# Two attention streams, one core: where VectorE prepares the latents, turns the side bank, and where the feed-forward modulation stands

## The reference, cut to what matters

```
hidden = (tanh(g / 2) + 1) * g * u          (twice silu(g) * u)
y     += w_down.T hidden
modh   = 0.1 * tanh(woa.T o) * (wa2.T x)     (once per item)
```

## Time and profile before

| | |
|---|---|
| three timed runs | 3610.35, 3618.64, 3619.7 us (median 3618.64) |
| profiled execution, its own time | 3609.97 us |
| its span, first to last instruction | 3608.2 us |
| mean granted TensorE clock | 0.957 of full speed |
| busy share of the span | PE 92%, PEld 75%, DVE 67%, ACT 54%, POOL 23% |

### The profile page before, as it was taken

One profiled execution on the slowest core, in us unless ns is written; L12 is line 12 of the kernel. 1 busy time (PEld: TensorE's weight loads), 2 busy tenths in 40 slices (PEclk: granted clock), 3 DMA queues, 4 the chain that ended last, 5 costly groups with the idle time before them and its releaser, 6 DMA issues. The chain is left out here.

```text
span 3608.2 us, 89141 instructions
## 1 busy us (share of the span) xinstructions
PE 3313.0 (92%) x34218; PEld 2701.3 (75%) x34218; DVE 2425.1 (67%) x7923; ACT 1959.2 (54%) x4767; POOL 817.1 (23%) x827
## 2 busy tenths in 40 slices
PE   6888896999999999999999868888979999999999
PEld 5676774888888888888888756766757777777787
DVE  4665654778777777777777535565656767777764
ACT  2444453666666666666666524454545555555553
POOL 2322221222222222222222222222210111111100
PEclk8998997999999999999999978898989999999999
DMA  5000000000000000000000040000000000000000
GB/s 223 1 1 1 1 1 18 14 20 20 20 20 20 20 20 20 20 20 20 20 20 20 8 151 1 1 1 1 1 1 1 1 1 1 1 1 7 4 7 10
DMA packets 51336, 66.83 MB, mean 19 GB/s; under 512 B 4962, under 2 KB 40290, under 8 KB 49378
## 3 DMA queue, kind: packets, MB, share of 16 engines
q1 hardware_dynamic: 50914, 61.13, 5.3%
HBM read 58.56 MB, written 2.56 MB: 17 GB/s over the span
## 5 line engine op out<-in xcount | busy, mean ns | idle before, releaser
L1286 DVE SCALAR_TENSOR_TENSOR d_acc<-d_raw,d_taps,d_acc 128x255 f32<-128x255 f32 (+2 forms) x1152 | 642.9, 599 | 146.2 <-ACT d_raw L1276 132.6
L2355 ACT ACTIVATE s_probs<-s_probs,s_nmax 128x128 f32<-128x128 f32 (+1 forms) x768 | 280.7, 443 | 187.9 <-DVE s_nmax L186 187.3
L1511 ACT COPY d_power<-bank 128x768 f32<-128x768 f32 x320 | 259.0, 809 | 218.7 <-PE bank L1504 218.7
L702 POOL TENSOR_TENSOR a_q<-a_rope 64x512 f32<-64x512 f32 x128 | 164.0, 1281 | 738.7 <-DVE a_rope L692 384.7
L186 DVE CUSTOM_DVE_ANT_0 a_area<-bank,mask 128x128 f32<-128x128 f32 (+1 forms) x512 | 160.3, 355 | 241.8 <-PE bank L720 239.4
L739 ACT ACTIVATE a_area<-a_area,a_nmax 128x128 f32<-128x128 f32 (+1 forms) x512 | 226.6, 444 | 165.2 <-DVE a_nmax L186 164.1
L1274 ACT ACTIVATE d_acc<-bank,d_tap_bias,d_taps 128x256 f32<-128x256 f32 x384 | 196.0, 561 | 166.5 <-PE bank L1255 158.7
L186 DVE CUSTOM_DVE_ANT_0 s_probs<-bank,mask 128x128 f32<-128x128 f32 (+1 forms) x768 | 220.9, 353 | 61.7 <-PE bank L2336 60.6
L765 ACT COPY a_area<-bank 128x512 f32<-128x512 f32 (+1 forms) x260 | 140.1, 578 | 138.7 <-PE bank L756 138.1
L2377 DVE COPY s_probsT<-bank 128x384 f32<-128x384 f32 x192 | 106.0, 555 | 119.9 <-PE bank L2363 117.7
L692 DVE TENSOR_TENSOR a_rope<-bank,a_sinT 32x512 f32<-32x512 f32 x256 | 177.4, 693 | 5.6
(11 more groups left out here) (267 smaller groups left out, 8783.3 us busy)
## 6 DMA issues: line engine op xcount, KB each, us to landing
d_alpha<-d_alpha_rows SPq DMA_DIRECT2D x64, 256.0 KB, 3.5
d_g_decay<-d_running_rows SPq DMA_DIRECT2D x32, 258.0 KB, 3.4
a_w_o<-in_a_w_o SPq DMA_DIRECT2D x2, 2048.0 KB, 16.5
a_area<-in_a_q_nope SPq DMA_DIRECT2D x2, 1536.0 KB, 8.2
x<-in_x SPq DMA_DIRECT2D x8, 256.0 KB, 16.3
d_wk<-in_d_wk SPq DMA_DIRECT2D x1, 2048.0 KB
d_wq<-in_d_wq SPq DMA_DIRECT2D x1, 2048.0 KB
d_wv<-in_d_wv SPq DMA_DIRECT2D x1, 2048.0 KB
```

Source lines behind the costliest of these rows:

```text
L702: nc.gpsimd.tensor_tensor(q[CL:P, n % 2], rope1[CL:P], rope2[CL:P], ALU.add)\
L1286: last = nc.vector.scalar_tensor_tensor(out=acc[:, r % 3, j, d:T], in0=raw[:, r % 2, j, 0:T - d], scalar=taps[:, r // 2, h, 3 - d:4 - d], ...
L1511: nc.scalar.copy(power[:], b_step[:, :, 0:3 * P]).then_inc(g.step_out, 1)
L2355: last = nc.scalar.activation(own, own, ACT.Exp, scale=-1.0, bias=nmax[:, s % 2, t, i:i + 1])
```

## The change

In `mla_sublayer`: (a) the last two transposes of `prep_late_pe` go to columns 256:512 of bank 6 (`b_qT1`) and no longer wait for ACT's copy of the first four; (b) on DVE `ln_normalize_dve` stands right behind the maxima, ahead of `oT_dve`; `prep_rms_dve` stands ahead of rope; the products of `prep_norm_dve` are split: token tile 0 at the end of p4, tile 1 in p5 ahead of rope, with the copy of the values; the statistics of p0 stand behind the reciprocal; (c) on POOL `prep_latent_pool` stands ahead of `rope_pool` in p4. In `small_stream`: (d) the transpose of the side bank stands after the first four of the eight maxima; (e) for feed-forward chunks that are due later than the first slot after their item, `modulate_pe` follows its gate and up products at once, `gate_act` stands behind the exponentials of the same slot, and `hidden_dve` ahead of `copy_dve` of the same slot. By the table `JOBS` that holds for 118 of 128 chunks, in 83 slots. No arithmetic is added or dropped.

```diff
@@ -385,6 +385,7 @@
         b_prep, b_q, b_s, b_pT, b_o, b_y = (core.bank[0], core.bank[1], core.bank[3:5],
                                             [core.bank[5], core.bank[2]], core.bank[6],
                                             core.bank[7])
+        b_qT1 = b_o[0:QL1, T:2 * T]
         PAIRS_ALL = NB * PAIRS
 
 
@@ -560,11 +561,12 @@
             nc.vector.tensor_scalar(ms_eps[:], ms[:], 1e-6, None, ALU.add)\
                 .then_inc(g.ms_eps_ready.sem, 1)
 
-        def prep_norm_dve(dve, it):
-            dve.wait_ge(*g.rms_ready(it, 1))
-            dve.wait_ge(*g.latT_in_psum(it, 0))
-            dve.wait_ge(*g.v_ready(it, 0))
-            for t in range(NT):
+        def prep_norm_dve(dve, it, tiles):
+            for t in tiles:
+                if t == 0:
+                    dve.wait_ge(*g.rms_ready(it, 1))
+                    dve.wait_ge(*g.latT_in_psum(it, 0))
+                    dve.wait_ge(*g.v_ready(it, 0))
                 nc.vector.scalar_tensor_tensor(
                     out=q_tok[:, t], in0=lat[:, t, 0:QL], scalar=inv_rms[:, t, 0:1],
                     in1=norm_w[:, 0:QL], op0=ALU.mult, op1=ALU.mult).then_inc(g.norm_ready.sem, 1)
@@ -639,14 +641,14 @@
             pe.wait_ge(*g.norm_ready(it, 2 * NT))
             pe.wait_ge(*g.kpe_ready(it, 1))
             pe.wait_ge(*g.lat_ready(it, NT))
+            pe.wait_ge(*g.latT_ready(it, 0))
             for t in range(NT):
                 nc.tensor.transpose(b_prep[:, t * P:(t + 1) * P], q_tok[:, t, 0:P], core.ident[:])
                 last = nc.tensor.transpose(b_prep[:, T + t * P:T + (t + 1) * P], k_tok[:, t],
                                            core.ident[:])
             last.then_inc(g.latT_in_psum.sem, 1)
-            pe.wait_ge(*g.latT_ready(it, 1))
             for t in range(NT):
-                last = nc.tensor.transpose(b_prep[0:QL1, t * P:(t + 1) * P], q_tok[:, t, P:QL],
+                last = nc.tensor.transpose(b_qT1[:, t * P:(t + 1) * P], q_tok[:, t, P:QL],
                                            core.ident[:])
             last.then_inc(g.latT_in_psum.sem, 1)
 
@@ -657,7 +659,7 @@
             nc.scalar.copy(latT[:, half].rearrange("p a t -> p (a t)"), b_prep[:, :])\
                 .then_inc(g.latT_ready.sem, 1)
             act.wait_ge(*g.latT_in_psum(it, 2))
-            nc.scalar.copy(qT1[0:QL1, half], b_prep[0:QL1, 0:T]).then_inc(g.latT_ready.sem, 1)
+            nc.scalar.copy(qT1[0:QL1, half], b_qT1).then_inc(g.latT_ready.sem, 1)
 
         def prep_late_dve(dve, it):
             dve.wait_ge(*g.norm_ready(it, 2 * NT))
@@ -910,7 +912,7 @@
                 if after_attention:
                     ternary_row_sum_dve(dve)
                 prep_rms_dve(dve, -1)
-                prep_norm_dve(dve, -1)
+                prep_norm_dve(dve, -1, range(NT))
                 prep_late_dve(dve, -1)
                 if after_attention:
                     ternary_weight_dve(dve)
@@ -927,28 +929,30 @@
                     if n < PAIRS_ALL:
                         max_dve(dve, n, 0)
                         max_dve(dve, n, 1)
+                    if it + 1 < NB and p == 1:
+                        ln_normalize_dve(core, dve, mla_at(it + 1), it + 1)
+                    if ternary_in(it) is not None and p == 6:
+                        ln_normalize_dve(core, dve, ternary_at(ternary_in(it)), ternary_in(it))
                     if n > 1:
                         oT_dve(dve, n - 2)
+                    if it + 1 < NB:
+                        if p == 4:
+                            prep_rms_dve(dve, it)
+                        if p == 5:
+                            prep_norm_dve(dve, it, [1])
+                            prep_late_dve(dve, it)
                     if n + 2 < PAIRS_ALL:
                         rope_dve(dve, n + 2)
+                    if n < PAIRS_ALL:
+                        recip_dve(dve, n)
                     if it + 1 < NB:
                         if p == 0:
                             mla_stats_dve(dve, it + 1)
-                        if p == 1:
-                            ln_normalize_dve(core, dve, mla_at(it + 1), it + 1)
                         if p == 4:
-                            prep_rms_dve(dve, it)
-                        if p == 5:
-                            prep_late_dve(dve, it)
-                    if n < PAIRS_ALL:
-                        recip_dve(dve, n)
-                    if it + 1 < NB and p == 4:
-                        prep_norm_dve(dve, it)
+                            prep_norm_dve(dve, it, [0])
                     if ternary_in(it) is not None:
                         if p == 5:
                             ternary_stats_dve(dve, ternary_in(it))
-                        if p == 6:
-                            ln_normalize_dve(core, dve, ternary_at(ternary_in(it)), ternary_in(it))
                         if p == 7:
                             ternary_add_dve(dve, ternary_in(it))
                     if n > 1 and p == 1:
@@ -1013,14 +1017,14 @@
                 for n in range(PAIRS_ALL):
                     it, p = n // PAIRS, n % PAIRS
                     pool.wait_ge(*g.q_rope_ready(0, min(n + 2, PAIRS_ALL)))
+                    if it + 1 < NB and p == 4:
+                        prep_latent_pool(pool, it)
+                        pool.wait_ge(*g.rms_ready(it, 1))
                     if n + 2 < PAIRS_ALL:
                         rope_pool(pool, n + 2)
                         pool.wait_ge(*g.q_rope_ready(0, n + 3))
-                    if it + 1 < NB:
-                        if p == 0:
-                            ln_rstd_pool(core, pool, mla_at(it + 1))
-                        if p == 4:
-                            prep_latent_pool(pool, it)
+                    if it + 1 < NB and p == 0:
+                        ln_rstd_pool(core, pool, mla_at(it + 1))
                     if ternary_in(it) is not None:
                         if p == 5:
                             ln_rstd_pool(core, pool, ternary_at(ternary_in(it)))
@@ -2339,10 +2343,10 @@
                                             skip_group_check=True)
             last.then_inc(g.scores_in_psum, 1)
 
-        def max_dve(dve, s):
+        def max_dve(dve, s, members_):
             need(dve, g.scores_in_psum, s + 1)
             need(dve, g.probsT_in_psum, GS * (s - 1))
-            for i in range(GS):
+            for i in members_:
                 for t, cols in ((0, slice(0, P)), (1, slice(P, 3 * P))):
                     masked_max_dve(core, probs[:, s % 2, i, cols], heads[:, i, cols], cols,
                                    nmax[:, s % 2, t, i:i + 1]).then_inc(g.max_ready, 1)
@@ -2395,13 +2399,15 @@
                                         tile_position=(0, 32 * i), skip_group_check=True)
             last.then_inc(g.pv_in_psum, 1)
 
-        def oT_dve(dve, s):
-
-            j, k = s // SETS, s % SETS
-            cols = slice(HD * (k % 2), HD * (k % 2 + 1))
+        def turn_dve(dve, s):
             need(dve, g.pv_in_psum, s + 1)
             need(dve, g.scaled, s)
             nc.vector.transpose(turned[:], b_side[:, 0:T]).then_inc(g.turned, 1)
+
+        def oT_dve(dve, s):
+
+            j, k = s // SETS, s % SETS
+            cols = slice(HD * (k % 2), HD * (k % 2 + 1))
             need(dve, g.turned, s + 1)
             nc.vector.reciprocal(recip[:], blocks(turned[:])[:, :, HD:HD + 1])\
                 .then_inc(g.recip_ready, 1)
@@ -2516,6 +2522,13 @@
         def steps_at(s):
             return [(j, step) for kind, j, step in JOBS.get(s, ()) if kind == FFN]
 
+        def modulated_early(s):
+
+            return [(j, step) for j, step in steps_at(s) if s > SETS * (j + 1)]
+
+        def modulated_late(s):
+            return [job for job in steps_at(s) if job not in modulated_early(s)]
+
         def out_at(s):
             return [j for kind, j, _ in JOBS.get(s, ()) if kind == ROTARY]
 
@@ -2548,6 +2561,8 @@
                         pv_pe(pe, s - 1)
                     for i, step in steps_at(s):
                         gate_up_pe(pe, i, step)
+                        if (i, step) in modulated_early(s):
+                            modulate_pe(pe, i, step)
                     if not steps_at(s):
                         y_pe(pe, s - 1)
                     if mod:
@@ -2559,7 +2574,7 @@
                         transposes_pe(pe, s)
                     if s < SLOTS and side_late(s):
                         side_pe(pe, j, k)
-                    for i, step in steps_at(s):
+                    for i, step in modulated_late(s):
                         modulate_pe(pe, i, step)
                     if steps_at(s):
                         y_pe(pe, s - 1)
@@ -2568,10 +2583,14 @@
             def _(dve):
                 for s in range(FIRST, ALL_SLOTS):
                     j, k = s // SETS, s % SETS
-                    for i, step in steps_at(s - 1):
+                    for i, step in modulated_late(s - 1):
                         hidden_dve(dve, i, step)
```

(10 more changed lines are left out.)

6 lines of the change are left out of this document (3 added, 3 removed).

## The result

| | before | after |
|---|---|---|
| median of timed runs | 3618.28 us | 3387.77 us (3386.09 to 3388.84) |
| ratio, with its 95% interval | | 0.9367 (0.935 to 0.9383) |
| profiled execution, its own time | 3609.97 us | 3388.84 us |
| its span | 3608.2 us | 3387.1 us |
| mean granted TensorE clock | 0.957 | 0.983 |

The kernel is 230.5 us faster by the medians and 221.1 by the profiled executions. The forecast of 3415 lies 27 us above the median; its range (3385 to 3465) holds the median, by 2.8 us at the lower end. I read the profiled pair: the two loops give 191.6 of the 221.1 us, the small stream 25.9, and 3.6 lie elsewhere, which is less than what lies between the stretches varies (from the end of the first loop to the start of the second it is 1622.7 us here and 1614.4 to 1621.1 in the kernels of the experiments).

The account below looks back on a forecast made before the run. PE was taken to bound all stages, losing time to waits and clock in the latent loops. Latent 192.8 - 9.3 - 7 = 176.5 plus small stream 18 gave 194.5 us off 3609.97: 3415 us, range 3385 to 3465.

Parts of the forecast that it names:

- The floor of a batch: Latent loops: eight slots of 5.78 us plus PE side work, 52.38 us against 68.33 measured; 192.8 us over both calls.
- DVE's stall: Slot p4: DVE stands 3.81 us for POOL's inverse root, PE then waits 3.62; both were to go.
- The worst case: Slot p4: POOL's whole latent chain begins only near 343.4, ends at 346.2, making the rotary add at most 0.2 us late.
- The port term: Latent p4: DVE products beside POOL's rotary add, 0.5 us knock-on in 14 batches, 7 us; by the lock rule 18.
- the likeliest case: Whole kernel: the forecast itself, 3415 us, counting on the latent clock staying full; chance 0.73.
- Rival 1: Latent loops: idle time goes but the clock stays low; 3498 us, or 3457 for half; chance 0.10.
- the rows I named: Small stream: PE's waits for `turned`, 10.7 us, all to end, and for `oT`, 14.7 us, half (7.3) to go.
- The new waits: Small stream: next slot's scores wait for `copy_dve` and ACT's copies; 3 us taken, bounds 0 and 25.
- Rival 2: Small stream: copies become the late ones, nothing gained and 25 us lost; 3458 us; chance 0.07.
- Rival 3: Latent p1 and p6: POOL's inverse root late for line 172 in 26 slots; slower, 3662 us at 5 us; chance 0.02.
- Rival 4: Latent p1, p5, p6: other waits take over, 2 us more per batch and its clock, 53 us; 3468; chance 0.08.
- Its lower bound: Whole kernel: added waits cost nothing (16 us) and half the small stream's remaining idle goes (14 us); 3385 us.

Follow-up runs that it names:

- the runs with one group undone: Changed kernel with normalised tokens behind rope again: 3468.3 us; changed kernel with POOL's latent work behind its rotary add again: 3451.23 us.
- the kernel without them: Changed kernel with copies ahead of gate tanh and hidden products in the second set of a rotary item: 3378.17 us, ratio 0.9334.

## Why the prediction was right, and where its sizes were off

**The bound and the floor.** The floor of a batch was put at 52.38 us. With no wait left it measures 52.03 (line 172 behind `oT`), the changed kernel has 52.58. Two side terms were too large: six late transposes cost 0.66 and not 0.83, four early ones 0.44 (6.21 - 5.77) and not 0.50, the early group twice a batch. That is 0.11 us for a transpose in either place, full width or half, where I had taken a row's length less 0.16 us of overlap. That makes 14 x 0.35 = 5 us of the 15 by which the loops did better (191.6 against 176.5). A misreading without weight: slice 7 of the clock stands at 7, so it is full from slice 8 and not from 7.

**(c) right.** The inverse root was forecast ready at 346.2 at worst, 5.8 us into its slot; it is ready at 4.14. DVE's stall and PE's 3.62 us are gone, and undoing it alone costs 63.4 us. The worst case was not needed, since POOL makes the rotary key products before the mean squares arrive.

**(b) right in place and in size.** With line 172 behind `oT` slot p1 lasts 6.21 and not 6.58, p6 6.21 and not 6.39. So the new wait of `pv` is 0.37 in p1 (taken 0.45) and 0.18 in p6 (taken 0.25): 14 x 0.37 + 12 x 0.18 = 7.3 against 9.3, and that kernel is 6.7 us faster.

**(a) mis-sized.** I priced it by PE's wait row, 0.68 us a batch, 9.5 us in 14 batches; the slots say 0.87 a batch, 12.2 us (16.2 by the medians, of which 3.8 lie in the untouched small stream by the profile). In the sum this did no harm, because the loops were priced as floor against measured batch.

**The port term is the step that failed.** I took 7 us for products beside POOL's rotary add, with 18 by the rule. The row shows the mechanism: 1.30 us for the product of 64 columns beside an add of 1.42, 0.28 elsewhere, and the product ends 0.08 us after the add (292.81 and 292.73). So the rule of the Trainium skill, page "SBUF — State Buffer", section on two separate sides, that the lock is held for a whole instruction, agrees with this trace, and my 0.5 was too small for the instruction. But its cost to the end is nothing: slot p5 lasts 6.43 us, and that is the 5.77 of a slot without side work and the 297.04 - 296.38 = 0.66 of the six transposes. DVE had more slack there than the lock takes. I had carried a stretched instruction into the sum without asking who waits behind it. Where slack is short it does cost: both pairs in p4 make 7.6 us. This term is 7 of the 15 us, the floor 5, the shorter waits of (b) 2.

**The clock came back in full,** as the likeliest case had it: 1.00 in both loops. Rival 1 (it stays) is out, and the runs with one group undone show it in between, at 0.97, with 30.7 us idle in the loop.

**Small stream: the rows I named came as forecast, and one gain was not in any of them.** Forecast 18, measured 26. PE's wait for `turned` fell by 8.7 of 10.7 us, the wait for `oT` by 7.0 of 14.7 (taken 7.3). The clock gave 2 x (2.9 - 1.2) = 3.4 us in slots 28 and 44 (taken 3). The failed step is the reading of the first row: I took PE's 10.7 us in 8 times as all that the turned bank costs, and 31 further slots lost 0.30 to 0.41 us to it, 10.6 us more, that only the weight loads show. The new waits, taken as 3, are 8.9 by the row of weight loads (10.6 less 1.7), and the seven slots that the kernel without them shortens give 8.9 as well. The rows cannot simply be added, since one slot can have several of these waits; the slots can: 10.6 us in the 31 slots, 10.3 in the nine first sets with a wait for `oT` (3.4 of it the clock), 5.4 in the ten slots where PE's own rows waited for the turned bank (13.2 us before, 2.5 of it at line 2181, which I had left out, and 2.0 after; the new waits take part of it back), 1.1 in slot 0, -1.3 in slot 46, -0.3 in the rest: 25.9. Slots 0 and 46 vary by that much between kernels with the same stream, so their two terms are the clock's and not the change's. Two errors of opposite sign, 10.6 and 6, partly cancel in the total: that 18 came near 26 is in part luck.

**Rivals.** Rival 2, late copies, is true in seven slots and worth 8.9 us (9.6 by the medians), not 25; it did not decide. Rival 3, the inverse root late for line 172: the row at 300.02 shows no wait for POOL. Rival 4, other waits in p1, p5 and p6: only the 7.3 us of (b).

**What stays open.** With (b), (c) undone the kernel with the new stream is at 3525.26, with the whole latent part undone at 3592.03. Of these 66.8 us (a) accounts for 12 to 16. The remaining 51 to 55 belong to what else differs, the split products, the earlier mean squares and the statistics behind the reciprocal, each with POOL's late root, and to the clock, 0.94 and 0.96 against 0.92 and 0.90; I ran no kernel that separates them. The split costs only 7.6 where the root is early. 3.6 us outside the stretches were not traced to a line. Which pause is followed by the lower clock, none of these runs explains.

**The range** held the median with 2.8 us to spare. Its lower bound was reached for the named reason only in part: the port term cost nothing, as it says, but `pv` did wait (7.3 us), and the floor, which the range left fixed, gave 5 us. Of the small stream it took 14 us more than forecast, and 8 came.

## To carry to other kernels

Ask of every move in a hand-written order who is queued behind the moved work and how much slack that queue has at that point: the latent part won 204 us mostly by moving short work ahead of long work that nobody was waiting for. Price a wait of the matrix engine by its weight loads and by the length from one repeated row to the next, since its own idle rows can show less than a third of it. When two edits remove one wait, expect that gain once; undo each alone and both together, since each alone showed about 2 us here and both 26.

## What the runs showed of the hardware

- A pause of one length has two prices in clock: 3.24 us without a drop and 3.23 us with one, 9.74 against 12.69 us for the slot, in one execution. The pause of 1.94 us was followed by the lower clock in slots 28 and 44 of the small stream before, and not in slot 68. At one place in the program it changes from execution to execution: after 1.54 us slot 46 lost the clock in one of nine kernels, after 2.01 us slot 76 in seven of nine (11.40 against 9.73 us). Waits that lengthen a slot by 0.37 and 0.87 us in every batch left the granted clock of the loop at 1.00.
- A DVE product is held up for nearly a whole POOL instruction: 0.28 us became 1.30 beside a POOL add, with its end 0.08 us behind that of the add, which itself took 1.42 us where it takes 1.27 alone. The same product for the next tile, 3 us later, takes 0.28 again.
- The idle time of PE's rows and that of PEld's differ by up to five times for the same wait (0.09 and 0.49 us for line 196 in an ordinary slot), and the slot's length goes with neither exactly: it shrank by 0.3.
